# Two-layer graph attention on one core: the first masks cut into parts, stage 2's exponentials moved between two passes, and two x loads moved ahead of a row load

## The reference

```python
def _L0_gnn_ref(h, adj, W, a):
    Wh = jnp.einsum('bni,io->bno', h, W)
    e1, e2 = Wh @ a[:OUT_F, 0], Wh @ a[OUT_F:, 0]
    e = e1[:, :, None] + e2[:, None, :]
    e = jnp.where(e > 0, e, 0.2 * e)                 # leaky relu
    scores = jnp.where(adj > 0, e, -9e15)
    attention = jax.nn.softmax(scores, axis=2)
    return jax.nn.elu(jnp.einsum('bnm,bmo->bno', attention, Wh))
# _L1_gnn_ref: the same with its own W, a, and without the elu
h = jnp.maximum(_layernorm(x), 0.0)
x = x + _L0_gnn_ref(h, adj, L0_gnn_W, L0_gnn_a)
h = jnp.maximum(_layernorm(x), 0.0)
x = x + _L1_gnn_ref(h, adj, L1_gnn_W, L1_gnn_a)
return x
```

## Time and profile before

| | |
|---|---|
| median of 3 runs | 298.2 us (297.83 to 298.87) |
| the profiled execution | 298.55 us, its span 296.8 us |
| PE busy | 289.6 us, 98% of the span |
| DVE busy | 267.6 us, 90% |
| ACT busy | 189.4 us, 64% |
| granted TensorE clock | 1.0 of full speed in the whole run |
| chain that ended last | PE 84%, DVE 6%, ACT 4%, DMA 2%, issue 2% |

### The profile page before, as it was taken

One profiled execution on the slowest core, in us unless ns is written; L12 is line 12 of the kernel. 1 busy time (PEld: TensorE's weight loads), 2 busy tenths in 40 slices (PEclk: granted clock), 3 DMA queues, 4 the chain that ended last, 5 costly groups with the idle time before them and its releaser, 6 DMA issues.

```text
span 296.8 us, 6604 instructions
## 1 busy us (share of the span) xinstructions
PE 289.6 (98%) x2557; PEld 287.2 (97%) x2557; DVE 267.6 (90%) x613; ACT 189.4 (64%) x491; POOL 49.5 (17%) x53
## 2 busy tenths in 40 slices
PE   7999998999999999999999999999999999999996
PEld 6889998999999999999999999999999999999996
DVE  4797897979999989999899989999899989978786
ACT  3377474884886839495694938768394958484310
POOL 2711005124012030303003030210303000400000
PEclk9999999999999999999999999999999999999999
DMA  7999954001592446813576334903467110101012
GB/s 223 415 405 410 406 213 164 0 2 46 170 333 95 144 141 215 352 41 122 196 227 273 143 109 155 363 17 144 144 189 309 68 77 1 73 0 71 2 73 71
DMA packets 16591, 48.97 MB, mean 165 GB/s; under 512 B 3632, under 2 KB 4784, under 8 KB 16560
## 3 DMA queue, kind: packets, MB, share of 16 engines
q1 hardware_dynamic: 15984, 48.16, 44.6%
q10 hardware_dynamic: 576, 0.39, 0.4%
HBM read 44.30 MB, written 4.24 MB: 164 GB/s over the span
## 4 chain that ended last, share of the span: by engine, by line
PE 84%; DVE 6%; ACT 4%; DMA 2%; issue 2%; POOL 1%; DVEq 0%; ACTq 0%
PE acc L950 65%; PE prj L893 8%; PE tp L832 4%; DVE pbuf L673 3%; PE acc L965 2%; DMA row_by_node<-r_rows 2%; ACT xn L376 1%; PE prj L896 1%; POOL rstd L281 1%; ACT accs L431 1%; ACT row_r L424 1%; PE prj L865 1%; PE tp L915 1%; PE prj L965 1%; PE prj L950 1%
## 5 line engine op out<-in xcount | busy, mean ns | idle before, releaser
L950 PE MATMUL acc<-wh,pbuf 128*128 128x129 f32 x1968 | 228.3, 275 | 2.0 <-DVE accs L682 1.4
L950 PEld LDWEIGHTS acc<-wh,pbuf 128*128 128x128 f32 x1968 | 224.1, 192 | 2.6 <-issue 2.0
L673 DVE SCALAR_TENSOR_TENSOR pbuf<-row_r,sqr,adj_sb 128x1024 f32<-128x1024 f32 x127 | 157.6, 1278 | 3.6 <-ACT row_r L424 2.5
L281 POOL TENSOR_TENSOR rstd<-vareps,neg_half 128x8 f32<-128x8 f32 x15 | 38.5, 2566 | 201.2 <-DVE vareps L586 201.2
L431 ACT ACTIVATE accs<-accs,rec 128x128 f32<-128x128 f32 x120 | 36.7, 389 | 46.9 <-DVE rec L692 46.9
L376 ACT ACTIVATE xn<-x_sb,shift,rstd 128x128 f32<-128x128 f32 x120 | 47.6, 479 | 0.0
L396 ACT ACTIVATE wh<-prj,wh 128x128 f32<-128x128 f32 x120 | 32.2, 370 | 0.1
L424 ACT ACTIVATE row_r<-row_by_node 128x1024 f32<-128x1024 f32 x12 | 25.3, 2106 | 8.4 <-DMA row_by_node<-r_rows 8.4
L893 PE MATMUL prj<-w_ext,hT 128*128 128x130 f32 x240 | 29.3, 275 | 0.0
L893 PEld LDWEIGHTS prj<-w_ext,hT 128*128 128x128 f32 x240 | 28.0, 191 | 0.0
L568 DVE BATCH_NORM_STATS2 stats<-x_sb 128x6 f32<-128x128 f32 x112 | 23.0, 279 | 0.0
(11 more groups left out here) (103 smaller groups left out, 153.7 us busy)
## 6 DMA issues: line engine op xcount, KB each, us to landing
adj_sb<-in_adj SPq DMA_DIRECT2D x64, 512.0 KB, 7.0
row_by_node<-r_rows SPq DMA_DIRECT2D x12, 512.0 KB, 4.3
x_sb<-in_x SPq DMA_DIRECT2D x7, 512.0 KB, 7.3
out_x<-x_sb SPq DMA_DIRECT2D x7, 512.0 KB, 2.7
x_sb<-in_x ACTq DMA_DIRECT2D x1, 256.0 KB, 3.4
x_sb<-in_x SPq DMA_DIRECT2D x1, 256.0 KB, 3.3
r_rows<-sqr SPq DMA_DIRECT2D x12, 4.0 KB, 2.2
out_x<-x_sb SPq DMA_DIRECT2D x1, 192.0 KB, 1.9
```

Source lines behind the costliest of these rows:

```text
L281: nc.gpsimd.tensor_tensor(rstd[:, :], vareps[:, :], neg_half[:, :], ALU.pow).then_inc(rstd_ready, 1)
L673: nc.vector.scalar_tensor_tensor(pbuf[:, t, :], row_r[:, n % 2, :], sqr[:, n % 2, 0, t:t + 1], adj_at(b, t), ALU.max, ALU.min).then_inc(p_ ...
L950: mm = nc.tensor.matmul(sum_at(k, s), pbuf[:, t, i * P:(i + 1) * P], wh[:, n % 2, t, :], start=(t == 0 and s == 0 and k < NB), stop=(t == ...
```

## The change

Four edits:

1. `masks_first`: the mask of tile 0 is made in four quarters, all from `tp`; the mask of tile 1 in two halves from `row_r`; `uniform_first` comes behind both. PE waits for each part on its own.
2. ACT copies the low half of the row once the first two quarters are made, scales one tile of `wh`, copies the high half once the fourth quarter is made, then scales the next tile.
3. `exps(2)` moves from behind both passes of the first elu to between them.
4. SP issues x of graphs 4 and 5 ahead of `load_row(2)` instead of behind it.

```diff
@@ SP
             for t in range(T):
                 load_adj(2, t)
-            load_row(2)
             load_x(4)
             load_x(5)
+            load_row(2)
@@ ACT
-            def copy_row_first():
-
-                act.wait_ge(r_spread, 2)
-                nc.scalar.activation(row_r[:, 0, N // 2:N], tp[:, N // 2:N],
-                                     ACT.Copy).then_inc(row0_ready, 1)
-                act.wait_ge(p_half, 1)
-                nc.scalar.activation(row_r[:, 0, 0:N // 2], tp[:, 0:N // 2],
+            def copy_row_first(h):
+
+                if h == 0:
+                    act.wait_ge(p_part, 2)
+                else:
+                    act.wait_ge(p_ready, 1)
+                cols = slice(h * (N // 2), (h + 1) * (N // 2))
+                nc.scalar.activation(row_r[:, 0, cols], tp[:, cols],
                                      ACT.Copy).then_inc(row0_ready, 1)
...
                 nc.scalar.activation(ex[:, :, :], hp, ACT.Exp).then_inc(ex_ready, 1)
+                if e == 0:
+                    exps(e + 2)
                 act.wait_ge(ex_ready, b + 1)
...
             scale_wh_first(range(1))
-            copy_row_first()
-            scale_wh_first(range(1, 3))
+            copy_row_first(0)
+            scale_wh_first(range(1, 2))
+            copy_row_first(1)
+            scale_wh_first(range(2, 3))
             normalise(1)
...
-                    exps(n + 1)
+                    if n > 1:
+
+                        exps(n + 1)
@@ DVE, masks_first
-                dve.wait_ge(adj_in[0][0], 16)
-                dve.wait_ge(r_spread, 1)
-                mask_half(lo, tp[:, lo]).then_inc(p_half, 1)
-                dve.wait_ge(row0_ready, 1)
-                mask_half(hi, row_r[:, 0, hi]).then_inc(p_ready, 1)
+                dve.wait_ge(adj_in[0][0], 16)
+                dve.wait_ge(sqr_ready, 1)
+                for q in range(4):
+                    cols = slice(q * (N // 4), (q + 1) * (N // 4))
+                    if q % 2 == 0:
+                        dve.wait_ge(r_spread, q // 2 + 1)
+                    nc.vector.scalar_tensor_tensor(
+                        pbuf[:, 0, cols], tp[:, cols], sqr[:, 0, 0, 0:1], adj_at(0, 0)[:, cols],
+                        ALU.max, ALU.min).then_inc(p_part if q < 3 else p_ready, 1)
+                dve.wait_ge(adj_in[0][1], 16)
+                for h in range(2):
+                    cols = slice(h * (N // 2), (h + 1) * (N // 2))
+                    dve.wait_ge(row0_ready, h + 1)
+                    nc.vector.scalar_tensor_tensor(
+                        pbuf[:, 1, cols], row_r[:, 0, cols], sqr[:, 0, 0, 1:2],
+                        adj_at(0, 1)[:, cols],
+                        ALU.max, ALU.min).then_inc(p_part if h == 0 else p_ready, 1)
...
-            masks(0, (1, 2, 3))
+            masks(0, (2, 3))
@@ PE, attend
-                    halved = n == 0 and t == 0
+                    in_parts = n == 0 and t < 2
...
+                        if in_parts and t == 0 and i in (0, 2, 4):
+                            pe.wait_ge(p_part, i // 2 + 1)
+                        if in_parts and t == 0 and i == 6:
+                            pe.wait_ge(p_ready, 1)
+                        if in_parts and t == 1 and i == 0:
+                            pe.wait_ge(p_part, 4)
+                        if in_parts and t == 1 and i == 4:
+                            pe.wait_ge(p_ready, 2)
```

More of the change, by code:

```diff
@@ L133, in gat_two_layers @@
         q_rstd_ready = sem("q_rstd_ready")
-        p_half = sem("p_half")
+        p_part = sem("p_part")
         sqr0_ready = sem("sqr0_ready")
@@ L646, in exp_args @@
                                         ALU.mult).then_inc(args_ready, 1)
-            def mask_half(cols, row):
-                return nc.vector.scalar_tensor_tensor(pbuf[:, 0, cols], row, sqr[:, 0, 0, 0:1],
-                                                      adj_at(0, 0)[:, cols], ALU.max, ALU.min)
             def masks_first():
-                lo, hi = slice(0, N // 2), slice(N // 2, N)
                 dve.wait_ge(adj_in[0][0], 16)
-                dve.wait_ge(r_spread, 1)
-                mask_half(lo, tp[:, lo]).then_inc(p_half, 1)
-                dve.wait_ge(row0_ready, 1)
-                mask_half(hi, row_r[:, 0, hi]).then_inc(p_ready, 1)
+                dve.wait_ge(sqr_ready, 1)
[14 more added lines that the diff above has]
+                        ALU.max, ALU.min).then_inc(p_part if h == 0 else p_ready, 1)
             def masks(n, tiles):
@@ L936, in attend @@
                         pe.wait_ge(wh_ready, T * n + T)
-                    halved = n == 0 and t == 0
-                    if halved:
-                        pe.wait_ge(p_half, 1)
-                    else:
+                    in_parts = n == 0 and t < 2
+                    if not in_parts:
                         pe.wait_ge(p_ready, T * n + t + 1)
@@ L943, in attend @@
                         k, s = place(n, i)
-                        if halved and i == T // 2:
+                        if in_parts and t == 0 and i in (0, 2, 4):
+                            pe.wait_ge(p_part, i // 2 + 1)
+                        if in_parts and t == 0 and i == 6:
                             pe.wait_ge(p_ready, 1)
+                        if in_parts and t == 1 and i == 0:
+                            pe.wait_ge(p_part, 4)
+                        if in_parts and t == 1 and i == 4:
+                            pe.wait_ge(p_ready, 2)
                         if t == 0 and s == 0 and n > 0 and k < NB:
```

## The result

The changed kernel takes 301.93 us in the median of 7 runs (299.33 to 302.17), the kernel before 298.2; the ratio is 1.0087, with a 95% interval of 1.0047 to 1.0126. (The ratios in this document lie near the ratio of the means. That of the two medians here is 1.0125.) So it is slower, by about 1%, and by more than was forecast: 301.93 lies above the range of 297.7 to 300.6. The seven times fall in two groups. Three are 299.33, 299.40 and 300.01 with a granted TensorE clock of 1.0; four are 301.93 to 302.17 with 0.994. The profiled execution is one of the four, 301.93 us with a span of 300.1.

A forecast was written before the change was run, and what follows sets the result against it. PE was taken as the bound, with gains possible only where it stands, ahead of stage 2. The row arriving 1.1 us later moves the median from 298.2 to 299.3 us, other delays hidden; range 297.7 to 300.6.

The forecast's parts named there:

- the sum: Start of stage 2: row in 1.1 us later, PE starting at 53.5 instead of 52.43, median 299.3 us.
- little changed between there and the end: From PE's start of stage 2 at 53.5 on, PE's idle time stays about as before.
- the term for the clock: PE's work behind the longer stop ahead of stage 2: no clock cost was stated or added.
- No rival: Cases beside the forecast: store not held up 0.13, row load pays back 0.24, slow row load 0.17, dear masks no own chance.
- Edits 1 and 2: First masks: PE starts 0.25 us earlier, stage 1's transposes come 0.3 later; +0.2 us for stage 1, no gain.
- A quarter's spacing of 0.41: Tile 0's mask on DVE: quarters start 0.41 us apart, each taking 0.49; spacing bounds 0.37 to 0.75.
- the +0.2: All of stage 1 runs 0.2 us later because of the masks made in parts.
- Edit 3: First elu: exponentials done at 39.93 instead of 40.69, store issued 0.75 us earlier; DVE's 0.55 us delay hidden.
- Lost in the queue: Store of stage 2's row: the 0.75 us from earlier exponentials is lost behind the x loads, and 2.34 us more.
- Edit 4, the store: SP's queue: store of stage 2's row lands with the x loads at about 44.45; row load issued at 44.47.
- Edit 4, the row load: Stage 2's row load, with no x loads behind it, takes 3.7 us instead of 4.95.
- the store isn't held up: Rival ahead of stage 2: store lands at 41.35, PE starts 0.95 us earlier, time 297.2 us; chance 0.13.

The follow-up runs named there:

- e3: The changed kernel with 18 identity transposes filling PE's stop ahead of stage 2; median 300.0 us.
- e7: The kernel before with only the masks in parts and the copies and `uniform` moved; median 298.66 us, ratio 1.0008.
- e1: The changed kernel with stage 2's row load ahead of the two x loads again; median 298.63 us, ratio 1.0013.
- e2: The kernel before with only the two x loads moved ahead of stage 2's row load; median 301.56 us, ratio 1.0098.
- e8: The changed kernel with one x load ahead of stage 2's row load and one behind; median 299.53 us, ratio 1.0043.
- e4: The changed kernel with the store of stage 2's row issued from ACT's queue instead of SP's; median 300.47 us.
- e9: The changed kernel with x loads issued once stage 2's row landed, and 12 identity transposes ahead of stage 1's transposes; median 298.28 us, ratio 0.9983.
- e6: The kernel before with only `exps(2)` moved between the first elu's passes; median 298.98 us, ratio 1.0.
- e5: The kernel before with `exps(2)` between the elu passes and x loads issued once stage 2's row landed; median 298.11 us, ratio 0.9983.

## Why the prediction was wrong

**The step that failed** is in the sum: "PE's idle time ahead of stage 2 grows from 1.4 to about 2.3." The stop came out so, at 2.37 us. But the sum prices it by its length alone, and the pieces behind it keep their time ("little changed between there and the end"): the term for the clock is nothing, without a reason. I took the granted clock of 1.0 from the kernel before as if it held behind any stop. Behind the longer one 32 pieces took 5.45 us in place of 3.81, 1.64 more; four of seven executions are in the group with the fallen clock, and the median is one of them. No rival had it. e3 shows it: the stop filled, the fall gone, the late start kept. The rest of the mechanism, the store held up and the start 1.43 us later, was right.

By its own steps otherwise:

- **Edits 1 and 2.** PE 0.25 us earlier at first and the transposes 0.3 later: 0.23 and 0.37. A quarter's spacing of 0.41: four took 1.66, so (1.66 - 0.49)/3 = 0.39. `args` of stage 2 ended at 39.92 against 39.48, of which 0.3 belong to this execution's later start: the +0.2 held. e7's ratio of 1.0008 fits no gain.
- **Edit 3.** `sqr` at 39.95 (39.72 forecast), the store at 40.20, 0.5 earlier than before and 0.75 less the late start. `add_elu` waited for the second pass and began at 41.39 in place of 40.61. Lost in the queue, as said; and in the kernel before there was little to win, because its store's 1.40 us were not those of a nearly empty queue either: it landed 0.24 us behind the last adjacency load.
- **Edit 4, the store.** Landing forecast 44.45, measured 40.20 + 4.65 = 44.85; the row load issued at 44.87 (44.47 forecast). The size held, the reason only in part: it is held by the x loads (e1, e2, e8), but not only because it stands behind them on SP's queue (e4).
- **Edit 4, the row load.** 3.7 forecast, 3.67 measured, in part by luck. I gave the whole 1.25 us to the absence of the x loads. By the rows of the kernel before, loads issued right behind cost some 0.7 us (an estimate: 4.3 to 4.6 against 3.3 to 3.8). The rest is the fetch: in the change it ran from 43.35 to 44.28, ahead of the load's issue at 44.87, and in the kernel before from 43.07 to 45.27, inside the load. That the late load missed it was not foreseen. The fit of the Trainium skill (DMA: Bandwidth & Descriptors, Anatomy of one DMA) that the prediction sets beside this is given there for DMAs issued through GpSimd; it makes 3.2 us, and this load, issued by SP, took 3.67.
- **The sum.** PE at 53.5 forecast, 53.86 measured; 0.29 of that is this execution's later start. Without the clock's fall, 1.43 us of later start make 299.6, and the three executions with a clock of 1.0 are 299.33, 299.40 and 300.01, against 299.3 forecast. (None of the three was profiled; that their stop was as long is inferred from these times.) Of the span's 3.3 us the remaining 1.9 are the 1.64 and small waits further on.

Of the rivals, "the store isn't held up" is refuted by the 4.65 us. The start of stage 2 that it gave, 51.5, is about what e9's profiled execution shows (51.45), though at 297.96 us and not 297.2; and that needed the x loads behind the row, not ahead.

What stays open: why the change kept its clock in 3 of 7 executions; where and why it fell once in e1 and once in e6, neither of them profiled; what made it fall in stage 0 of e4's profile; and through what the store from ACT's queue was held in e4.

## What to carry to other kernels

A wait that grows on the engine that bounds the kernel costs its own length and may cost the clock after it: before pricing a longer PE stop, look at the granted clock of the windows behind the stops that are there, and count a second group of times as a case of its own. Bulk loads issued ahead of a small latency-bound transfer hold it up by their full length (1.3 us per 512 KB here), and issuing it from another queue did not help; put the bulk behind the transfer, or make SP wait for its landing. When one of two similar transfers is slow, look at the queue of kind "instruction" in its window as well as at its neighbours. And profile executions of both groups before trusting one: a profile is one execution.

## What the runs showed of the hardware that I had not expected

- A stop of 2.37 us on PE was followed, over a microsecond after work had begun again, by some 3.4 us at half clock; the same kernel stayed at the full clock in 3 of 7 executions. Eighteen idle transposes in the stop kept the clock in 6 of 6. In e4's profile the clock fell in stage 0 as well, from about 13.2 to 16.6 us, with PE busy ahead of it.
- A 4 KB store issued from ACT's queue took 5.2 us beside 1 MB of loads on SP's queue, and landed 0.17 us after the second of them.
- PE's instruction fetch, 16 KB on one DMA engine, can hold up a sixteenth of a 512 KB load and with it the whole: in e5 the last eight packets ran only once the fetch had ended, and the load took 5.3 us. Loads without a fetch took 3.3 to 3.8 in the kernel before.
